# Graph attention over a dense adjacency matrix: order, mask place and low-part engine in the first two row tiles

## What is computed

```
h      = max(layernorm(x), 0)
g      = inlayer2 @ W.T + b ;  f1 = g @ w1 + b1 ;  f2 = g @ w2 + b2
logits = leaky_relu(f1[:, None] + f2[None, :], 0.01) + (-1e9 where adj == 0)
out    = x + softmax(logits, axis=-1) @ h
```

## Time and profile before

| what | value |
|---|---|
| median of three runs | 1439.55 us |
| the profiled execution, whole | 1441.07 us |
| its span (first to last instruction) | 1439.3 us |
| PE busy | 1407.1 us (98%) |
| DVE busy | 1276.7 us (89%) |
| ACT busy | 614.6 us (43%) |
| POOL busy | 264.2 us (18%) |
| DMA, mean rate over the span | 210 GB/s |

### The profile page before, as it was taken

The page is one execution under the profiler, slowest core; times in us unless marked ns, Lnnn a source line. Parts: engine busy times, 40 slices in busy tenths (PEclk is TensorE's granted clock), DMA queues, the critical chain, the costliest instruction groups (busy, mean ns, idle before and its releaser), DMA issues.

```text
span 1439.3 us, 33339 instructions
## 1 busy us (share of the span) xinstructions
PE 1407.1 (98%) x12623; PEld 1246.2 (87%) x12623; DVE 1276.7 (89%) x1315; ACT 614.6 (43%) x713; POOL 264.2 (18%) x266
## 2 busy tenths in 40 slices
PE   8589999999999999999999999999999999999998
PEld 7468888888888888888888888888888888888887
DVE  5999989898898989989899898998989989898894
ACT  2895443444343444434444344443434434344330
POOL 0692011111110111111111011111101101111110
PEclk9799999999999999999999999999999999999999
DMA  9979999999999999999999999999999999999940
GB/s 293 322 178 217 233 232 234 233 224 212 211 211 207 217 209 209 215 208 210 210 215 210 208 215 209 210 216 208 210 208 217 210 209 216 207 212 212 211 106 12
DMA packets 110184, 302.43 MB, mean 210 GB/s; under 512 B 11732, under 2 KB 44628, under 8 KB 110164
## 3 DMA queue, kind: packets, MB, share of 16 engines
q1 hardware_dynamic: 100080, 289.52, 89.7%
q10 hardware_dynamic: 10084, 12.65, 3.0%
HBM read 293.73 MB, written 8.39 MB: 210 GB/s over the span
## 4 chain that ended last, share of the span: by engine, by line
PE 96%; DMA 2%; ACT 1%; DVE 1%; ACTq 0%; issue 0%; SPq 0%
PE acc L1055 62%; PE acc L1057 31%; PE rp L1010 2%; DMA adj_sb<-in_adj_dram 1%; ACT h_f L589 0%; ACT rp L573 0%; PE rp L1024 0%; DMA w<-in_L_gnn_w_dram 0%; PE small L997 0%; PE rp L1018 0%; DVE wgt L844 0%; ACT mask L573 0%; PE small L1069 0%; ACTq L343 0%; ACTq L348 0%
## 5 line engine op out<-in xcount | busy, mean ns | idle before, releaser
L1055 PE MATMUL acc<-H,wT 128*128 128x257 f16 x8192 | 1354.9, 273 | 9.2 <-DVE H L824 6.0
L1057 PE MATMUL acc<-H,wT 128*128 128x257 f16 x4096 | 1119.5, 273 | 0.0
L1055 PEld LDWEIGHTS acc<-H,wT 128*128 128x128 bf16 x8192 | 801.9, 98 | 110.9 <-issue 7.1
L854 DVE STREAM_TRANSPOSE wT<-wgt 128x1024 f32<-128x1024 f32 x512 | 634.7, 1241 | 130.2 <-PE acc L1057 130.1
L573 ACT ACTIVATE mask<-adj_sb 128x1024 bf16<-128x1024 int32 x504 | 521.2, 1055 | 535.4 <-DVE wgt L844 437.0
L844 DVE SCALAR_TENSOR_TENSOR wgt<-b_word,c_word,mask 128x1024 f32<-128x1024 f32 x504 | 627.4, 1257 | 1.0 <-ACT mask L573 1.0
L1057 PEld LDWEIGHTS acc<-H,wT 128*128 128x128 f16 x4096 | 401.6, 98 | 50.3
L493 POOL TENSOR_TENSOR x_res<-o_room,x_res 128x256 f32<-128x256 f32 x63 | 66.7, 1059 | 1099.4 <-ACT o_room L580 1073.1
L580 ACT ACTIVATE o_room<-acc,r_den 128x256 f32<-128x256 f32 x63 | 29.9, 475 | 236.6 <-DVE r_den L873 236.6
L498 POOL TENSOR_TENSOR o_room<-o_room,x_res 128x256 f32<-128x256 f32 x63 | 80.9, 1284 | 5.2
L495 POOL TENSOR_SCALAR o_room<-h_mean,no_nb 128x256 f32<-128x256 f32 x63 | 58.2, 924 | 0.0
(11 more groups left out here) (93 smaller groups left out, 162.4 us busy)
## 6 DMA issues: line engine op xcount, KB each, us to landing
adj_sb<-in_adj_dram SPq DMA_DIRECT2D x504, 512.0 KB, 8.6
x_res<-in_x_dram SPq DMA_DIRECT2D x64, 128.0 KB, 4.0
out_dram<-o_room SPq DMA_DIRECT2D x63, 128.0 KB, 4.3
H<-in_x_dram ACTq DMA_DIRECT2D x16, 256.0 KB, 12.7
H<-in_x_dram SPq DMA_DIRECT2D x16, 256.0 KB, 13.0
adj_sb<-in_adj_dram ACTq DMA_DIRECT2D x8, 512.0 KB, 14.7
wgt<-in_L_gnn_inlayer_dram ACTq DMA_DIRECT2D x8, 256.0 KB, 9.7
wgt<-in_L_gnn_inlayer_dram SPq DMA_DIRECT2D x8, 256.0 KB, 10.1
```

The source lines that it names most:

```text
L854: nc.vector.transpose(wT[:, wT_slot(I, k), :, :].rearrange("p t (g r) -> p g t r", g=Q), wgt[:, wgt_slot(I, c), :, s * SQ:(s + 1) * SQ]).t ...
L1055: pe.matmul(acc[:, par, 0:DV], w_hi[:, slot, t, :], H[:, j, part, 0:DV], start=(j == 0 and part == 0), stop=False)
L1057: mm = pe.matmul(acc[:, par, 0:DV], w_lo[:, slot, t, :], H[:, j, 0, 0:DV], start=False, stop=(j == ROWS - 1))
```

## The change

Four things change, all of them within rows 0 and 1.

1. **Order.** Row 1's first chunk is loaded, masked and weighted ahead of row 0's second chunk. `two_rows` now has the order (0, c 0), (1, c 0), (0, c 1), (1, c 1) and serves for the masks too; `mask_order` and `nth_mask` are gone. In ScalarE's and VectorE's programs the masks and weights of (1, c 0) stand before those of (0, c 1), and TensorE's order becomes (1,0), (1,1), (1,2), (1,3), (0,4), (0,5).
2. **Loads.** SyncE and ScalarE issue row 1's chunk 0 first and row 0's chunk 1 after it.
3. **Place of masks.** The four masks of row 0's second chunk are written to `mask[:, 1]` in bf16 instead of to `rp` in fp32; row 1's masks of chunk 1 then wait for the weights that read that room.
4. **Unit 9.** `low_of_values(9)` moves from VectorE to GpSimd, behind unit 8's. `low_on_pool` and `wait_low` keep the counts.

```diff
--- before.py
+++ after.py
@@ -129,7 +129,7 @@
...
         acc_room = acc[:, :, :].rearrange("p a n -> p (a n)")
-        row0_mask = [[rp[:, 0, :], rp[:, 1, :], acc_room, rp[:, 0, :]], [rp[:, 1, :], rp[:, 0, :], rp[:, 1, :], rp[:, 0, :]]]
+        row0_mask = [rp[:, 0, :], rp[:, 1, :], acc_room, rp[:, 0, :]]
         small = ctx.enter_context(nc.psum_tensor("small", [P, 2, 512], F32))
         t_ps = small[:, 0, :]
         hm_ps = small[:, 0, 0:D]
@@ -277,14 +277,11 @@
...
-        mask_order = ((0, 0, 0), (0, 1, 0), (0, 2, 0), (0, 3, 0), (0, 0, 1), (0, 1, 1), (0, 2, 1),
-                    (1, 0, 0), (1, 1, 0), (0, 3, 1), (1, 2, 0), (1, 3, 0), (1, 0, 1), (1, 1, 1),
+        two_rows = ((0, 0, 0), (0, 1, 0), (0, 2, 0), (0, 3, 0), (1, 0, 0), (1, 1, 0), (1, 2, 0),
+                    (1, 3, 0), (0, 0, 1), (0, 1, 1), (0, 2, 1), (0, 3, 1), (1, 0, 1), (1, 1, 1),
                     (1, 2, 1), (1, 3, 1))
-        two_rows = ((0, 0, 0), (0, 1, 0), (0, 2, 0), (0, 3, 0), (0, 0, 1), (0, 1, 1), (1, 0, 0),
-                    (1, 1, 0), (1, 2, 0), (1, 3, 0), (0, 2, 1), (0, 3, 1), (1, 0, 1), (1, 1, 1),
-                    (1, 2, 1), (1, 3, 1))
-        strip_order = ((0, 0), (0, 1), (0, 2), (0, 3), (1, 0), (1, 1), (1, 2), (0, 4),
-                       (1, 3), (0, 5), (1, 4), (1, 5), (0, 6), (0, 7), (1, 6), (1, 7))
+        strip_order = ((0, 0), (0, 1), (0, 2), (0, 3), (1, 0), (1, 1), (1, 2), (1, 3),
+                       (0, 4), (0, 5), (1, 4), (1, 5), (0, 6), (0, 7), (1, 6), (1, 7))
         def first_two(I):
             return is_row(I, 0) or is_row(I, 1)
@@ -292,10 +289,6 @@
...
             return two_rows.index((I, g, c)) + 1 if first_two(I) else 8 * I + (Q * c + g + 1)
-        def nth_mask(I, g, c):
-            return mask_order.index((I, g, c)) + 1 if first_two(I) else 8 * I + (Q * c + g + 1)
         def nth_strip(I, k):
@@ -318,6 +311,16 @@
...
                 eng.wait_ge(h_ready, HALF * (n - before + 1))
+        low_on_pool = (0, 2, 4, 6, 8, 9, 10, 12, 14)
+        def wait_low(eng, n):
+            before = sum(m < n for m in low_on_pool)
+            if n in low_on_pool:
+                eng.wait_ge(lo_ready, before + 1)
+            else:
+                eng.wait_ge(lo_dve_ready, n - before + 1)
         def wait_slot(eng, n):
             if n == HR - 1:
@@ -325,7 +328,7 @@
...
                 wait_high(eng, m)
-                eng.wait_ge(lo_dve_ready if m % 2 else lo_ready, m // 2 + 1)
+                wait_low(eng, m)
         def wait_high(eng, n):
@@ -366,7 +369,7 @@
...
         def second_adj(eng, c, quadrants):
-            eng.wait_ge(m_ready, nth_mask(0, Q - 1, c))
+            eng.wait_ge(m_ready, nth_part(0, Q - 1, c))
             load_adj(eng, 1, c, quadrants)
         @block.sync
@@ -378,7 +381,6 @@
...
             load_x(sp, 4, 8, (0, 1))
-            first_adj(sp, 1, (0, 1))
             for i in range(2):
                 sp.dma_start(x_res[:, i, :], x_rows[i]).then_inc(x_loaded[i], 16)
@@ -390,8 +392,10 @@
...
                     if n % Q == Q - 1 and not is_row(I, ROWS - 1):
-                        sp.wait_ge(m_ready, nth_mask(I, Q - 1, n // Q))
+                        sp.wait_ge(m_ready, nth_part(I, Q - 1, n // Q))
                         load_adj(sp, I + 1, n // Q, (0, 1) if is_row(I, 0) else (0, 2, 1, 3))
+                    if n == Q - 1 and is_row(I, 0):
+                        first_adj(sp, 1, (0, 1))
                     if n == NS - 1 and not (is_row(I, 0) or is_row(I, 1) or is_row(I, 2)):
                         store_row(I - 2, par, I)
                     if n == Q - 1 and is_row(I, 3):
@@ -526,6 +530,7 @@
...
             low_of_values(8)
+            low_of_values(9)
             D_column(4)
             rstds(7)
             affine(7)
@@ -561,15 +566,15 @@
...
                 if is_row(I, 0) and n >= 3:
-                    act.wait_ge(p_ready, nth_part(0, *((0, 0), (1, 0), (3, 0), (0, 1), (1, 1))[n - 3]))
+                    act.wait_ge(p_ready, nth_part(0, 0, 0))
                 if is_row(I, 1):
-                    act.wait_ge(p_ready, 1)
+                    act.wait_ge(p_ready, nth_part(0, g, c))
                 if is_row(I, 2):
                     act.wait_ge(p_ready, nth_part(1, g, c))
                 if not (first_two(I) or is_row(I, 2)):
                     act.wait_ge(p_ready, 8 * I + (n - 7))
                 act.wait_ge(adj_loaded[c], 16 * Q * (I + 1))
-                place = row0_mask[c][g] if is_row(I, 0) else mask[:, c, g * CQ:(g + 1) * CQ]
+                place = row0_mask[g] if is_row(I, 0) and c == 0 else mask[:, c, g * CQ:(g + 1) * CQ]
                 nc.scalar.activation(place, adj_sb[:, c, g * CQ:(g + 1) * CQ], ACT.Relu,
                                      scale=M_SCALE).then_inc(m_ready, 1)
@@ -644,12 +649,12 @@
...
             mask_part(0, 1, 0)
-            first_adj(act, 1, (2, 3))
             mask_part(0, 2, 0)
             mask_part(0, 3, 0)
             values(1)
+            second_adj(act, 0, (2, 3))
+            first_adj(act, 1, (2, 3))
             high_of_values(1)
-            second_adj(act, 0, (2, 3))
             values(2)
             high_of_values(2)
             values(4)
@@ -657,19 +662,19 @@
...
             high_of_values(5)
-            mask_part(0, 0, 1)
+            mask_part(1, 0, 0)
             values(6)
             high_of_values(6)
             high_of_values(7)
+            mask_part(1, 1, 0)
+            mask_part(1, 2, 0)
+            mask_part(1, 3, 0)
+            mask_part(0, 0, 1)
             mask_part(0, 1, 1)
             mask_part(0, 2, 1)
-            mask_part(1, 0, 0)
-            mask_part(1, 1, 0)
             mask_part(0, 3, 1)
+            values(8)
             second_adj(act, 1, (2, 3))
-            mask_part(1, 2, 0)
-            mask_part(1, 3, 0)
-            values(8)
             high_of_values(8)
             values(9)
             high_of_values(9)
@@ -679,12 +684,12 @@
...
             mask_part(1, 2, 1)
+            mask_part(1, 3, 1)
             values(12)
             high_of_values(12)
-            mask_part(1, 3, 1)
             values(13)
+            high_of_values(13)
             values(14)
-            high_of_values(13)
             high_of_values(14)
             high_of_values(15)
             mask_part(2, 0, 0)
@@ -835,12 +840,12 @@
...
             def weights(I, g, c):
-                dve.wait_ge(m_ready, nth_mask(I, g, c))
+                dve.wait_ge(m_ready, nth_part(I, g, c))
                 if first_two(I) and c == 1 and g == 0:
                     dve.wait_ge(t_ready, nth_strip(I, 3))
                 if is_row(I, 2) and c == 0 and g == 0:
                     dve.wait_ge(t_ready, nth_strip(0, 7))
-                shown = row0_mask[c][g] if is_row(I, 0) else mask[:, c, g * CQ:(g + 1) * CQ]
+                shown = row0_mask[g] if is_row(I, 0) and c == 0 else mask[:, c, g * CQ:(g + 1) * CQ]
                 nc.vector.scalar_tensor_tensor(out=wgt[:, wgt_slot(I, c), g, :], in0=b_word[:, c * CQ:(c + 1) * CQ],
                                                scalar=c_word[:, bass.ds(Q * I + g, 1)],
                                                in1=shown, op0=ALU.max, op1=ALU.min).then_inc(p_ready, 1)
@@ -898,26 +903,25 @@
...
             low_of_values(5)
-            weights(0, 0, 1)
-            raw_stats(60, 64)
-            variance(7)
-            weights(0, 1, 1)
-            low_of_values(7)
             weights(1, 0, 0)
             weights(1, 1, 0)
+            low_of_values(7)
             weights(1, 2, 0)
             weights(1, 3, 0)
             turn(1, 0)
+            weights(0, 0, 1)
+            turn(1, 1)
+            weights(0, 1, 1)
+            turn(1, 2)
+            raw_stats(60, 64)
+            variance(7)
             weights(0, 2, 1)
-            turn(1, 1)
+            turn(1, 3)
             weights(0, 3, 1)
-            turn(1, 2)
-            low_of_values(9)
             turn(0, 4)
-            turn(1, 3)
             low_of_values(11)
+            turn(0, 5)
             weights(1, 0, 1)
-            turn(0, 5)
             weights(1, 1, 1)
             weights(1, 2, 1)
             weights(1, 3, 1)
@@ -1046,8 +1050,9 @@
...
                     wait_high(pe, 2 * k + 1)
-                    for part in (lo_ready, lo_dve_ready, D_column_ready):
-                        pe.wait_ge(part, k + 1)
+                    wait_low(pe, 2 * k)
+                    wait_low(pe, 2 * k + 1)
+                    pe.wait_ge(D_column_ready, k + 1)
                 slot = wT_slot(I, k)
                 for t in range(TS):
                     j = TS * k + t
@@ -1085,8 +1090,8 @@
...
             products(1, 1, 2)
+            products(1, 1, 3)
             products(0, 0, 4)
-            products(1, 1, 3)
             products(0, 0, 5)
             sum_of_values(4)
             sum_of_values(5)
```

## The result

The changed kernel takes 1444.19 us (median of 7 runs, 1442.95 to 1446.01); the kernel before took 1439.86 us beside it (7 runs, 1439.13 to 1441.16). The ratio is 1.0029, 95% interval 1.0019 to 1.0039: slower, by slightly more than the 0.2% named above. The forecast was 1441.2 us; the result lies inside the range and on the side that had a chance of 0.25. The profiled execution took 1442.95 us (span 1441.2), against 1441.07 us before.

What follows compares the result with a forecast made beforehand. TensorE was taken to bound the kernel, so only the moment from which it runs unbroken counts. -3.85 + 5.05, rounded to +1.3, became +1.7 with the tie: 1439.55 + 1.7 = 1441.2 us; range 1436.2 to 1444.8, own range 1439.9 to 1442.6.

Steps and rivals of the forecast that it cites:

- The exclusion: GpSimd instructions and VectorE instructions with two SBUF inputs shut each other out, each for its whole length.
- the near tie: Weights (1,1,0) might get ahead of low part 6, 0.15 us deciding; sum then +2.3, given four in ten.
- 1.6 us of it are lost again: If TensorE's clock also falls after its gap of 80.04 to 83.35, 1.6 us of the gain at (1,0) goes.
- The gaps behind: TensorE waits ahead of (1,3), (0,4), (0,5) and (1,4): 0.8, 0.8, 2.35 and 1.1 us, 5.05 lost.
- Column 5: GpSimd's copy of the denominator column, done at 104.0 instead of 99.1, holding up strip (0,5) by 2.35 us.
- The mark: Start of strip (1,4) on TensorE, same work behind it in both kernels: forecast 109.05 against 107.72 before.
- the very sum: Net shift of strip (1,4)'s start: -3.85 + 5.05 = +1.2, made +1.3 by rounded steps.
- with a gap too short for the lower clock another 1.59: At strip (1,0), TensorE keeps full clock, gaining 1.59 us besides starting 2.26 earlier.
- rival C: Row 1's chunk lands late, at 77.7 instead of 72.7, delaying all masks: +4.6 us, 1444.2; chance 0.10.
- A, the order pays: GpSimd works in VectorE's gaps and delays nothing; (1,4) starts at 104.3: -3.4 us, 1436.1; chance 0.17.
- B, GpSimd starves: VectorE keeps the port through back-to-back instructions, strip (0,3) starts at 86.0: +5 to +7.5, about 1446; chance 0.12.
- D: No effect: stalls trade places exactly, -1 to +0.3 us; chance 0.08.

Runs made afterwards that it cites:

- before_again: The kernel before, unchanged, run once more for a second profiled trace: 1439.94 us.
- warm_before: The kernel before with useless matmuls filling TensorE's gaps ahead of strips (0,3) and (1,0): 1440.74 us, ratio 1.0004 to the kernel before.
- psum2: The changed kernel with two masks of row 0's second half, (0,0,1) and (0,1,1), back in PSUM: 1444.00 us, ratio 1.0021 to the kernel before.
- row1psum2: The changed kernel with row 1's masks (1,0,0) and (1,1,0) put in PSUM: 1443.14 us, ratio 1.0014 to the kernel before.
- psum4_l9: Changed kernel with four masks in PSUM and low part 9 on VectorE: 1442.46 us; its _warm version adds nine useless matmuls ahead of (1,4): 1440.97 us.
- warm_after: The changed kernel with ten useless matmuls ahead of strip (0,3) and ten ahead of (1,4): 1444.19 us, ratio 1.0026 to the kernel before.
- b_sbuf: The kernel before with only the masks of row 0's second half moved from PSUM to SBUF: 1442.48 us, ratio 1.0009 to the kernel before.
- b_low9pool: The kernel before with only low part 9 moved from VectorE to GpSimd: 1439.97 us, ratio 0.9995 to the kernel before.
- low9dve: The changed kernel with low part 9 back on VectorE: 1444.10 us, ratio 1.0023 to the kernel before.

## Why the prediction was right, and where it wasn't

**The mechanism.** Right, and shown. The exclusion between GpSimd and VectorE's instructions with two SBUF inputs carries the loss in the traces: 0.9 us of stretch before, 5.3 after, 4.5 with the masks' place alone, 1.4 with the new order and four masks in PSUM. The ledger of VectorE closes: +4.4 stretch, -1.1 for low part 9, -1.0 for idle time that is gone (1.1 to 0.1) gives +2.3. The later start of the first strip of all in this trace (69.06 to 69.64, 0.6 us) makes it 2.9, and turn(1,4) ends 3.0 us later. Against before_again it closes to 0.2 us: the stretch and low part 9 make +3.3, the start is 0.5 us earlier, and turn(1,4) ends 3.0 later.

**The steps.** Low part 7 and strip (0,3) came as forecast (83.42 for 83.35), though by the other turn: low part 6 went ahead of weights (1,0,0), not behind; the two waits have the same length, so the near tie made no difference. Part of the agreement is luck: VectorE's low part 5 started 0.63 us later than in the trace that I worked from, and from there strip (0,3) came 0.56 us sooner than I had it. turn(1,0) ended at 86.84 (forecast 86.8). (1,0) started at 88.80 instead of 87.05, since the clock fell after the gap of 2.61 us, the case that I had named with "1.6 us of it are lost again"; but it didn't carry through. The gaps behind came smaller and elsewhere: 0.48, 0, 0.55 and 2.44 us where I had 0.8, 0.8, 2.35 and 1.1. Column 5 was done at 102.26, not at 104.0, and GpSimd held up no strip; its waits came out shorter at values(11) (3.12 us for four), and VectorE paid instead, at the variance and at low part 11. The mark is at 109.59 (forecast 109.05). Counted from the start of strip (0,0), it is at 38.66 us in the first trace of before and at 39.95 after: +1.3, the very sum. That is luck: parts of the working erred both ways, and counted from the same point before_again has its mark at 36.40, which makes +3.5.

**The step that failed** is "with a gap too short for the lower clock another 1.59". The traced execution of before carried a lower clock at (1,0), and I took it for part of the kernel. before_again shows (1,0) at the full clock, its (2,0) starts 1.14 us earlier, and warm_before, which keeps the clock up, is no faster than before. A gain can't be had from a loss that the median doesn't hold, as its spans say: I brought the sum from the profiled execution down to the median and kept the credit, so the lower clock was counted twice. At the mark it was worth 1.14 us (107.72 to 106.58); without it the same working says 1439.55 + 1.7 + 1.1 = 1442.4 us. What was measured, 1444.19, is 4.3 us above the median beside it where I had 1.7, and 1.6 us outside the forecast's own range (1439.9 to 1442.6, where its stated terms give 1440.4 to 1442.4). It is within the whole range, and it happens to be the number of rival C, 1444.2, whose late chunk is in neither trace of the changed kernel. Against before_again the changed kernel's (2,0) is 3.0 us later (126.73 to 123.72), which is what the span of both traces says too (1441.2 to 1438.2).

**What stays open.** The medians differ by 3.7 to 4.3 us and the traces by 3.0. No trace shows an execution of the changed kernel at its median of 1444; both took about 1443.0. Three things seen in other traces could do it: the lower clock at (1,4), as in psum2, row1psum2 and psum4_l9 (1.5 to 1.7 us); row 1's chunk landing late, as in warm_after and psum4_l9_warm; and a late start of the first strips (strip (0,0) started between 68.88 and 70.18 over all traces), which the kernel before takes up in VectorE's wait for masks and the changed kernel has no wait left to take up. The first alone isn't enough, as far as the runs go: warm_after fills the gap ahead of (1,4), and its median is the same. How often each occurs in the changed kernel isn't known.

**The rivals.** A, the order pays: refuted; its best case, psum4_l9_warm, is the kernel before. B, GpSimd starves: seen only where it no longer counts, at the 6.16 us for four values; GpSimd got its turns, and (0,3) started at 83.42 and not at B's 86.0. C, a late chunk: not in the two traces of the changed kernel, but half of it in warm_after, so its 0.10 was too little for a cause that can come in some executions. D: no. In the sum over its parts, the masks' place costs 1.3 to 2.1 us (b_sbuf), low part 9 on GpSimd nothing that can be told, and the new order costs 1.5 us by its last gap, where that brings the lower clock (psum4_l9 against psum4_l9_warm).

The Trainium skill, page "SBUF — State Buffer", section "SBUF: two separate sides", names a second kind of VectorE instruction that takes the shared pair, beside those with two SBUF inputs: one in a 2-port performance mode. The variance of 1.75, 2.86 and 2.87 us, which has one input, agrees with that if it ran in such a mode, which no row shows; I had used only the half of the rule about two inputs.

No version beats the kernel before. The best idea left, b_low9pool, is at 0.9995 with an interval that includes 1. Masks in bf16 in PSUM, where its rooms would hold twice as many as of fp32, weren't tried.

## What to carry to other kernels

Before a loss in a profile is credited as a gain, a second trace of the same kernel has to show it: one profiled execution can hold a stretch at a lower clock that the median doesn't. Where the second operand of a VectorE instruction moves from PSUM to SBUF, count the GpSimd instructions beside it at full length against VectorE, and the reverse: here a low part of 2.14 us made weights of 1.27 us last 3.16. And look for the last wait in the chain: here a gain ahead of it was taken up by VectorE, which ended it, while a lower clock behind it was paid in full (1.5 us).

## What wasn't expected of the hardware

- A VectorE instruction with one input of 128x8, 0.17 us by itself, waited for GpSimd as well: it took 1.75 us behind the rest of one low part, and 2.86 and 2.87 us where two low parts of GpSimd ran back to back (4.22 us for both in warm_after). It did not come in between the two. The reverse was mixed: beside VectorE's row of four weights GpSimd's values came in after the second of them and again after the fourth (2.55 us each instead of 0.55).
- Gaps of TensorE of the same length went either way: after 1.91 (psum2), 2.14 (b_low9pool, at (0,3)), 2.45 (row1psum2, psum4_l9) and 2.61 us (after, at (0,3)) the granted clock was down; after 2.14 (before, at (0,3)), 2.12 and 2.13 (before_again), 2.44 (after, at (1,4)), 2.45 (low9dve, at (1,4)) and 2.71 us (row1psum2, at (1,3)) it stayed at 1.00. A strip at the lower clock takes some 4.3 us instead of 2.65.
- Row 1's chunk, issued at the same place of the same queues, let its first mask start at 72.67 in one execution of the new order and at 74.16 and 74.85 in executions of its relatives.
